# Layer 2 of a four-layer kernel: the side branch's first norm in search rounds 7 to 11, a quarter of the branch ahead of the experts, shared down products in the last rounds

## The reference

```python
# side branch ("attn" of layer 2)
attn_out = cumprod(cos(xn.reshape(..., 16, 8)), axis=-1)
x1  = layer_norm(xn + attn_out, gamma1, beta1)          # the first norm
q   = cumprod(cos(x1[..., :16]), axis=-1)               # small circuit
h   = relu(q @ w1.T + b1)                               # 16 -> 512
s   = layer_norm(x1 + h @ w2.T + b2, gamma2, beta2)
# experts ("ffn" of layer 2)
scores = softmax(xn @ gate_w.T).T                       # 16 experts
w, idx = top_k(scores, 256)                             # 256 tokens each
eo  = (gelu(xg @ Wg.T) * (xg @ Wu.T)) @ Wd.T * w        # xg = xn[idx]
out = scatter_add(eo at idx) + (gelu(xn @ Sg.T) * (xn @ Su.T)) @ Sd.T
x   = x + s * silu(out)
```

## Time and profile before

| What | us |
|---|---|
| Median of 3 runs | 1841.46 (1840.22 to 1844.49) |
| The profiled execution's own time | 1838.87 |
| Its span | 1837.1 |
| PE busy in the span | 1629.7 (89%) |
| DVE busy | 1306.8 (71%) |
| ACT busy | 1090.9 (59%) |
| POOL busy | 1083.6 (59%) |

### The profile page before, as it was taken

One profiled execution on the slowest core, in us unless ns is written; L12 is line 12 of the kernel. 1 busy time (PEld: TensorE's weight loads), 2 busy tenths in 40 slices (PEclk: granted clock), 3 DMA queues, 4 the chain that ended last, 5 costly groups with the idle time before them and its releaser, 6 DMA issues. The chain is left out here.

```text
span 1837.1 us, 32207 instructions
## 1 busy us (share of the span) xinstructions
PE 1629.7 (89%) x12270; PEld 1368.0 (74%) x12270; DVE 1306.8 (71%) x2709; ACT 1090.9 (59%) x2241; POOL 1083.6 (59%) x1038
## 2 busy tenths in 40 slices
PE   6999999999999999989985898965799368989897
PEld 4888888888888888877774777754688246666676
DVE  6888887878787878854346177859743888887782
ACT  3677767767777767755544565552444345666666
POOL 4888899999999999994017374643666410101011
PEclk9999999999999999999988999987799678999999
DMA  3000000000100000000003500013256200000000
GB/s 95 13 3 1 16 1 15 1 15 1 39 1 1 2 1 1 1 30 1 1 10 113 141 24 2 2 24 100 57 138 142 69 0 1 2 1 2 1 2 24
DMA packets 64089, 50.28 MB, mean 27 GB/s; under 512 B 10544, under 2 KB 55760, under 8 KB 63808
## 3 DMA queue, kind: packets, MB, share of 16 engines
q1 hardware_dynamic: 53328, 34.59, 6.5%
q0 software_dynamic: 8496, 12.59, 3.2%
q10 hardware_dynamic: 2112, 1.05, 0.2%
HBM read 37.72 MB, written 10.49 MB: 26 GB/s over the span
## 5 line engine op out<-in xcount | busy, mean ns | idle before, releaser
L756 POOL TENSOR_TENSOR dtl<-dts,dth 128x512 fp32r<-128x512 f32 x256 | 353.4, 1380 | 20.5
L686 DVE TENSOR_REDUCE nm<-PS 128x1 f32<-128x1024 f32 x256 | 311.4, 1217 | 28.6 <-PE PS L206 27.6
L2044 ACT ACTIVATE ET_a<-PS 128x256 f32<-128x256 f32 (+2 forms) x512 | 220.2, 497 | 126.1 <-PE PS L1957 79.0
L754 POOL CAST dth<-dts 128x512 fp32r<-128x512 f32 x256 | 234.5, 916 | 50.4 <-ACT dts L613 49.3
L204 PE MATMUL PS<-xh,yh 128*128 128x512 f32 x512 | 225.5, 440 | 9.4 <-ACT XNT L606 5.0
L1856 POOL TENSOR_SCALAR_AFFINE_SELECT ET_a<-ET_a 128x1024 f32<-128x1024 f32 x32 | 35.0, 1094 | 303.6 <-ACT ET_a L2044 303.6
L147 PE MATMUL PS<-C,XN 128*128 128x128 f32 x1120 | 175.6, 282 | 42.0 <-DVE XN L199 38.2
L206 PE MATMUL PS<-xh,yl 128*128 128x512 f32 x512 | 204.4, 399 | 0.0
L205 PE MATMUL PS<-xl,yh 128*128 128x512 f32 x512 | 204.2, 399 | 0.0
L606 ACT ACTIVATE XNT<-PS,nm 128x1024 f32<-128x1024 f32 x128 | 142.8, 1115 | 72.2 <-DVE nm L686 71.3
L613 ACT ACTIVATE dts<-PS 128x512 f32<-128x512 f32 x256 | 152.6, 598 | 46.3 <-POOL dtl L756 44.4
(11 more groups left out here) (427 smaller groups left out, 4283.9 us busy)
## 6 DMA issues: line engine op xcount, KB each, us to landing
e_wg<-in_WgT SPq DMA_DIRECT2D x16, 256.0 KB, 2.7
e_wu<-in_WuT SPq DMA_DIRECT2D x16, 256.0 KB, 3.0
e_wd<-in_WdT SPq DMA_DIRECT2D x16, 256.0 KB, 4.0
m_x_rows<-m_xs SPq DMA_DIRECT2D x1, 1472.0 KB, 5.1
m_xs<-m_x_rows SPq DMA_DIRECT2D x5, 256.0 KB, 4.2
m_y_rows<-m_xs SPq DMA_DIRECT2D x5, 256.0 KB, 3.9
X<-in_L_attn_X SPq DMA_DIRECT2D x2, 512.0 KB, 4.5
wqn<-in_L_attn_Wq SPq DMA_DIRECT2D x8, 128.0 KB, 2.2
```

Of the source, the lines that this page charges most:

```text
L686: e.tensor_reduce(self.nm[:, half, i:i + 1], self.S[half], AX.X, MAX, negate=True).then_inc(*self.top.up((g, half)))
L754: e.tensor_copy(hi, src).then_inc(*ts.up((g, g4, "h")))
L756: e.tensor_tensor(lo, src, f(hi), SUB).then_inc(*ts.up((g, g4, "l")))
L2044: e.activation(dst, src, ACT.Exp, scale=self.SC, bias=0.0).then_inc(*self.ex.up(it))
```

## The change

The search keeps its rounds, with other fillers. Statistics go to rounds 7 to 10 and moments to round 11. The down products of the shared expert are cut into halves: five halves, (0,0), (1,0), (0,1), (1,1), (0,2) as (half, quarter), go into rounds 10 to 14, and the other three follow "take". "x1" stands in round 12. "q" comes after the last half. A one-element gelu follows the sine on ACT. The two copies into `q3` move from expert 1 to a step "q3" behind pick 0. The gathers of experts 0 to 2 move on POOL from before the sine's wait to behind `q3l`. The parts of side quarter 0, but for its "addT", run on PE and ACT behind pick 0 and before the loop ("ahead"). Pick 1 moves into expert 0 of the loop. The remaining 19 parts are spread over experts 1 to 12 with every fifth place left free, and the second norm's statistics of quarter 0 move from expert 4 to 5. The blocks that walk the script move, in the PE and ACT programs, behind the definition of `side`; this is left out below.

```diff
@@ plan
-        self.side, slots = [], []
-        for c in range(4):
-            for part in ([("first", 0, c)], [("up", 0, c), ("up", 1, c)], [("up", 2, c), ("up", 3, c)],
-                         [("down", 0, c), ("down", 1, c)], [("down", 2, c), ("down", 3, c)], [("addT", 0, c)]):
-                slots.append(part)
-                self.side += part
-        self.slots = {(1 + n // 2, 1 + 2 * (n % 2)): part for n, part in enumerate(slots)}
+        work = lambda c: [[("first", 0, c)], [("up", 0, c), ("up", 1, c)], [("up", 2, c), ("up", 3, c)],
+                          [("down", 0, c), ("down", 1, c)], [("down", 2, c), ("down", 3, c)]]
+        turned = lambda c: [("addT", 0, c)]
+        self.ahead = work(0)
+        slots = work(1) + [turned(0), turned(1)] + work(2) + [turned(2)] + work(3) + [turned(3)]
+        self.side = [u for part in self.ahead + slots for u in part]
+        self.slots = {(1 + m // 2, 1 + 2 * (m % 2)): part for m, part in ((n + n // 4, part) for n, part in enumerate(slots))}
...
-            if 10 <= b < 14:
-                out.append(("stats", b - 10, 0))
-            elif b == 14:
+            if 7 <= b < 11:
+                out.append(("stats", b - 7, 0))
+            elif b == 11:
                 out.append(("moments", 0, 0))
+            if b >= 10:
+                out.append(("sdown", b % 2, (b - 10) // 2))
+            if b == 12:
+                out.append(("x1", 0, 0))
             out.append(("digit", b, 0))
-        out += [("x1", 0, 0), ("q", 0, 0), ("take", 0, 0), ("take", 1, 0), ("take", 2, 0), ("sdown", 0, 0), ("sdown", 0, 1)]
-        out += [("hot", 0, n) for n in range(3)]
-        out += [("pick", 0, 0), ("sdown", 0, 2), ("pick", 0, 1), ("sdown", 0, 3)]
-        out += [("hot", 1, n) for n in range(3)] + [("pick", 1, 0), ("pick", 1, 1)]
+        out += [("take", 0, 0), ("take", 1, 0), ("take", 2, 0), ("sdown", 1, 2), ("sdown", 0, 3), ("sdown", 1, 3), ("q", 0, 0)]
+        out += [("hot", 0, n) for n in range(3)] + [("pick", 0, 0), ("pick", 0, 1), ("q3", 0, 0)]
+        out += [("ahead", n, 0) for n in range(len(self.ahead))] + [("hot", 1, n) for n in range(3)]
         self.script = out
-        self.later = {}
+        self.later = {(0, 1): ("pick", 1, 0), (0, 3): ("pick", 1, 1)}
...
@@ pool
-        for x in range(3):
-            gather(x)
         q.wait_ge(self.sin, "q")
...
         e.tensor_tensor(self.q3[:, :, 32:48], qq, f(self.qh[:, :, :]), SUB).then_inc(*c.up("q3l"))
+        for x in range(3):
+            gather(x)
...
@@ pe
             elif what == "sdown":
                 q.wait_ge(self.sh_mul, (c, 1))
-                o = self.bank_free(q, x)
-                for j in range(4):
+                o = self.bank_free(q, x) if n == 0 else k.bank(self.slot["sdown", 0, c])
+                for j in (2 * n, 2 * n + 1):
...
-                t.then_inc(*self.sh_down.up(c))
+                if n == 1:
+                    t.then_inc(*self.sh_down.up(c))
...
+            elif what == "ahead":
+                for u in self.ahead[n]:
+                    side(u)
...
@@ act
                 e.activation(s, s, ACT.Sin, scale=1.0, bias=self.hp[:, :]).then_inc(*self.sin.up("q"))
+                e.activation(k.sm[:, 5, 15:16], k.cst("ones")[:, 0:1], ACT.Gelu, scale=1.0, bias=0.0)
+            elif what == "q3":
+                q.wait_ge(self.qc, "qh")
+                q.wait_ge(self.on_pool, "q3")
+                for j in range(2):
+                    e.activation(self.q3[:, :, 64 * j:64 * j + 16], f(self.qh[:, :, :]), ACT.Copy).then_inc(*self.q3h.up(j))
+            elif what == "ahead":
+                for u in self.ahead[n]:
+                    side(u)
...
-                if (x, m) == (1, 0):
-                    q.wait_ge(self.qc, "qh")
-                    q.wait_ge(self.on_pool, "q3")
-                    for j in range(2):
-                        e.activation(self.q3[:, :, 64 * j:64 * j + 16], f(self.qh[:, :, :]), ACT.Copy).then_inc(*self.q3h.up(j))
...
@@ dve, norm
-            if x in (4, 7, 10, 13):
-                n = 4 * ((x - 4) // 3) + m
+            if x in (5, 7, 10, 13):
+                n = 4 * (5, 7, 10, 13).index(x) + m
```

More of the change, by code:

```diff
@@ L2434, in plan @@
                 uses += [x + ("g",), x + ("u",)]
-            elif x[0] == "sdown":
+            elif x[0] == "sdown" and x[1] == 0:
                 uses.append(x)
@@ L2705, in side @@
                 t.then_inc(*self.side_pe.up(x))
+        for x in self.script:
+            what, n, c = x
+            cs = slice(512 * c, 512 * c + 512)
+            if what == "begin":
+                begin()
+            elif what == "count":
+                q.wait_ge(self.find, ("count", n, 2))
+                e.matmul(B1[:, 0:3], same, self.cn3[:, :], start=True, stop=True).then_inc(*self.find_pe.up(n))
+            elif what == "sup":
+                ms = slice(128 * n, 128 * n + 128)
+                q.wait_ge(self.in_s, 2)
+                q.wait_ge(self.on_pool, "sl")
+                q.wait_ge(p.low, c)
+                xs = p.xh[:, cs], p.xl[:, cs]
+                og = self.bank_free(q, x + ("g",))
+                mm3(e, og, (self.sh[:, 0, ms], self.sl[:, 0, ms]), xs, True, True)
+                ou = self.bank_free(q, x + ("u",))
+                mm3(e, ou, (self.sh[:, 1, ms], self.sl[:, 1, ms]), xs, True, True).then_inc(*self.sh_up.up((c, n)))
+            elif what == "sdown":
+                q.wait_ge(self.sh_mul, (c, 1))
+                o = self.bank_free(q, x) if n == 0 else k.bank(self.slot["sdown", 0, c])
+                for j in (2 * n, 2 * n + 1):
+                    for m in range(2):
+                        t = e.matmul(o[:, 128 * j:128 * j + 128], self.shb[c][:, m, 128 * j:128 * j + 128], self.sd[:, m, :], start=m == 0,
+                                     stop=m == 1)
+                if n == 1:
+                    t.then_inc(*self.sh_down.up(c))
+            elif what == "take":
+                take(n)
+            elif what == "pick":
+                pick(n, c)
+            elif what == "ahead":
+                for u in self.ahead[n]:
+                    side(u)
         def turn(x):
@@ L2801, in side @@
                     *self.side_act.up(x))
+        for x in self.script:
+            what, n, c = x
+            cs = slice(512 * c, 512 * c + 512)
+            if what == "begin":
+                q.wait_ge(self.gate, "sub")
+                e.activation(self.SC[:], self.SC[:], ACT.Exp, scale=1.0, bias=0.0).then_inc(*self.gate_exp.up("e"))
+            elif what == "sup":
+                q.wait_ge(self.sh_up, (c, n))
+                e.activation(self.shb[c][:, n, :], k.bank(self.slot[x + ("g",)]), ACT.Gelu, scale=1.0, bias=0.0).then_inc(
+                    *self.sh_gelu.up((c, n)))
+            elif what == "sdown" and n == 1:
+                q.wait_ge(self.sh_down, c)
+                e.activation(k.G[:, 4 * c:4 * c + 4, :], k.bank(self.slot["sdown", 0, c]).rearrange("p (j d) -> p j d", j=4), ACT.Copy).then_inc(
+                    *self.sh_out.up(c))
+            elif what == "sin":
+                s = self.S[:, :, :].rearrange("p n d -> p (n d)")
+                q.wait_ge(self.circ, ("cos", 4, 1))
+                e.activation(s, s, ACT.Sin, scale=1.0, bias=self.hp[:, :]).then_inc(*self.sin.up("c"))
+            elif what == "x1":
+                q.wait_ge(self.qc, "shift")
+                for i in range(NT):
+                    t = e.activation(self.X1[:, i, :], self.S[:, i, :], ACT.Identity, scale=k.sm[:, 3, i:i + 1], bias=self.shift[:, i:i + 1])
+                    if i % 4 == 3:
+                        t.then_inc(*self.x1.up(i // 4))
+            elif what == "q":
+                s = self.q[:, :, :].rearrange("p n d -> p (n d)")
+                q.wait_ge(self.qc, ("qcos", 4))
+                e.activation(s, s, ACT.Sin, scale=1.0, bias=self.hp[:, :]).then_inc(*self.sin.up("q"))
+                e.activation(k.sm[:, 5, 15:16], k.cst("ones")[:, 0:1], ACT.Gelu, scale=1.0, bias=0.0)
[7 more added lines that the diff above has]
+                    side(u)
         def turn(x):
```

55 lines of the change are left out of this document (removed).

## The result

| | before | after |
|---|---|---|
| Median of 16 runs each, us | 1842.7 (1840.06 to 1847.25) | 1850.32 (1847.83 to 1855.43) |
| The profiled execution's own time (span) | 1838.87 (1837.1) | 1851.28 (1849.5) |

The ratio is 1.0043, 95% interval 1.0035 to 1.0051: slower by 7.6 us, where 2.1 were forecast. The direction was right, the size was not, and 1850.3 lies outside the range of 1838.2 to 1849.0. (Of the distance to the 1843.6 forecast, 1.2 us lie in the starting point: the prediction had three runs of the kernel before, with a median of 1841.46.)

What follows compares the result with a forecast made beforehand. Prediction: DVE bounds the search, PE the expert loop. First up product 5.2 us later, loop 3.1 shorter, so 2.1 us slower: 1843.6 against a median of 1841.46, range 1838.2 to 1849.0.

Steps and rivals of the forecast that it cites:

- Last digit: End of the search: 2.1 us later, because statistics and moments move into rounds with other filler or leave rounds needing it.
- To the last halves: From last digit to first remaining half on PE: 4.45 us as before, plus 0.5 for POOL's work beside DVE.
- Three halves: Last three halves of shared down products on PE, after "take": 4.9 us with a low-clock start, 3.1 at high clock.
- Sine to the end of q3: POOL's products up to the low part, beside DVE's one-hots of group 1: 4.7 us, where 4.27 was measured before.
- To the first down product: Transposes, copy, lifts and relus through PE and ACT after q3: 5.1 us, or 4.2 at the high clock.
- Four down products: Down products run ahead of the loop on PE: 4.6 us, between 3.44 at high clock and 6.9 at low.
- The loop: Expert loop on PE: 4.80 us of quarter 0's parts leave, 1.67 of pick 1 enter, so 3.13 us shorter.
- A: Rival, chance 0.20: halves keep PE's clock up and the ahead chain starts warm; -3.3 to -0.5 us, about 1839.5.
- D: Rival, chance 0.06: q3 ready so early that PE waits only for the gather and starts warm; -4.8 us, 1836.7.
- C: Rival, chance 0.10: in "take" five DVE instructions each wait about 0.7 us for POOL; +5.1 us in total, 1846.5.
- B: Rival, chance 0.22: low clock through the ahead down products, over 5.5 us, if PE waits over 4; +5 to +6.6, about 1847.
- The forecast's own slow end: Every term before the loop taken at its slow value: first up product at 1328.5, sum +6.6 us.

Runs made afterwards that it cites:

- b3: Kernel before plus only the cut down products, five halves in rounds 10 to 14 and three behind pick 0: ratio 1.0000, layer 221.56 us.
- b1: Changed kernel keeping only the new search and the halves; ahead parts, pick 1, POOL's order and q3 copies undone: ratio 1.0016, layer 223.17 us.
- a1: Changed kernel with the sine moved ahead of the last three halves in ACT's order: ratio 1.0021, layer 222.75 us.
- b2: Changed kernel without the parts run ahead and without pick 1 in the loop; gathers stay behind q3: ratio 1.0028, layer 224.45 us.
- a2: Changed kernel with DVE's one-hots of group 1 held until POOL has written q3l: ratio 1.0029, layer 226.35 us.
- d1: Changed kernel with the second norm's statistics of quarter 0 in expert 6 instead of 5: ratio 1.0057, layer 228.42 us.
- c1: Changed kernel with the sine ahead of the last halves and first-norm statistics in rounds 9 to 12: ratio 1.0016, layer 225.33 us.
- a3: Changed kernel with 18 filler matmuls on PE between pick 0 and the parts run ahead: ratio 1.0043, layer 226.78 us.
- c2: Changed kernel with the sine ahead of the last halves and only transposes and lifts run ahead, down products in the loop: ratio 1.0007, layer 220.89 us.

## Why the prediction was wrong in size

Each step by its own terms, in us from the layer's start or as a duration:

| Step | Forecast | Measured | Off |
|---|---|---|---|
| Last digit | 64.84 | 65.27 | +0.4 |
| To the last halves | 5.0 | 5.31 | +0.3 |
| Three halves | 4.9 | 5.33 | +0.4 |
| Copy, table, sine | 2.5 | 2.5 | 0 |
| Sine to the end of q3 | 4.7 | 5.93 | +1.2 |
| To the first down product | 5.1 | 5.60 | +0.5 |
| Four down products | 4.6 | 5.21 | +0.6 |
| To the first up product | 1.2 | 1.05 | -0.1 |
| The loop | 110.0 | 111.44 | +1.4 |

The sum is 4.8: 3.3 ahead of the loop and 1.4 in it, on top of the 2.1 forecast, which is the 6.9 by which the layer grew.

**What held.** The path held step by step. Fillers taken from rounds that needed them cost 2.5 us (2.1 forecast); the sine did not come earlier, since it stands behind the last halves; the gathers, 6.5 us later, were covered; the first up product is what the side chain releases. "x1", the halves within the rounds (b3) and the small gelu bound nothing. b1, a1 and b2 each undo a part that the prediction had named.

**The steps that failed.** The terms were the right ones, but three groups of them were sized too small. (1) The products beside the one-hots: "beside the one-hots of group 1 on DVE I take 4.7" allowed 0.4 us of stretching; it was 1.9 (a2), of which the low part gave 0.3 back (0.73 instead of 1.05). The section on POOL beside DVE looked only at "take", where two of DVE's instructions were stretched, by 0.5 and 0.4 us (the second scan 1.15 instead of 0.67, the sum of positions 0.83 instead of 0.43), in all 0.9 us from digit to halves against 0.5 taken. The pair that the change itself creates was not priced with the one pair of which a row stood there (1.82 against 1.28, rows 5). (2) The low clock: for the down products I took 4.6, a third of the way from the high to the low value. They took 5.21, and 5.2 to 6.7 in the other runs that have them ahead. Nearly all of the halves lay at the low clock too (5.33 against 4.9), and so did the transposes (1.10) and lifts (0.81 each), with 5.60 against 5.1 for the way to the first down product. (3) The loop: I subtracted what moves out at its own duration and added pick 1 at its own. The chain before shows the up product behind a grid or small product at 0.63 instead of 0.43 (its row at 1335.03, one line below those quoted): 0.4 us for the two. The first piece took 0.70 instead of 0.43, 0.3; the third wait is 0.3 to 0.5 (d1). These pieces are read from rows; but for the wait no run tests them. The last 0.3 us I can't place.

**The rivals.** A (the clock stays up) is refuted by the clock of 0.50 from 1292 to 1310, and again from 1316 to 1328. D (all hidden) is refuted by PE's wait of 6.03 us for q3. C (five instructions of DVE wait for a POOL step, 3.5 us) is refuted in its size: two of the five waited, 0.9 us together. B, the low clock through the down products, has its place right and in a1, a2, c1 and d1 its price too (over 5.5 us); in the profile of the changed kernel they took 5.21, so by its own sign it did not come, though the total lies nearer to it than to my forecast. Its condition, a wait of over 4 us for q3, was met (6.03 us) but is not the cause alone (a3). The forecast's own slow end, +6.6, held most of the terms that failed, but not the loop's 1.4 us, and the range gave 5.4 us on that side. All of the terms but one failed in the same direction; 1.5 of the 4.8 us are pieces of PE between search and loop that met the low clock.

One more reading was wrong, without a cost here: "The rows of expert 0 are there at 1313.1 + 6.8" took the 6.8 us as the gather's own. They hold a large transfer beside it (b2), and the rows came 3.9 us after the first issue.

What stays open: how much of the difference between 5.21 and 6.66 is the moment the profile was taken in, and the loop's last 0.3 us.

## What to carry to other kernels

A gap on the engine that the kernel goes by isn't worth its length: small dependent steps in it ran at a granted clock of 0.50 here, and the first product of a lift, 0.50 us at full clock (a3), took 0.81. Moving work from a full, warm loop into a gap pays only as far as it fits beside a wait that stays; here transposes and lifts did so (c2, level with the kernel before), down products did not (a1). Before a time between two events is carried over to another order, look what else lay in it: the 6.8 us from gather to turn held another transfer and, on PE, pick 1. Before work on POOL and on DVE is put side by side, look for the one pair of like instructions that the trace shows together and use its stretching for all of them; and look behind which step the released engine then stands in its list, since POOL's early argument waited 7.6 us for a copy.

## What I had not expected of the hardware

The granted clock fell without a long pause: with PE busy 1.1 to 1.3 of every 2 us and no gap over 0.78 us from 1318.3 to 1322.8, it went from 1.00 to 0.50 (a3), and it was at 0.50 too in rounds 11 to 14, where halves filled 5.06 of 6 us, after 0.45 busy in the two us from 1290. The same down products after nearly the same pause took 5.21 us in one profile and 6.66 in another (after, d1). The gathered rows of expert 0 came 3.9 to 4.6 us after the first issue in twelve kernels, and 6.8 us in the one where a transfer of 1024 KB ran beside the second half. POOL's seven products took 2.64 to 4.71 us, by what DVE did beside them.
